# A graph attention over source nodes rewritten: keys spread by a load, scores by a broadcast weight, one-hots that carry the edge weight

## What is computed

```python
feat = jnp.concatenate([x[src], edge_weights, x[dst]], axis=1)      # 64 + 16 + 64 = 144
h = jax.nn.relu(feat @ W_att1.T + b_att1)                            # 144 wide
scores = (h @ W_att2.T + b_att2)[:, 0]
m = jax.ops.segment_max(scores, src, num_segments=num_nodes)
e = jnp.exp(scores - m[src])
denom = jax.ops.segment_sum(e, src, num_segments=num_nodes)
msg = jax.ops.segment_sum(e / denom[src] * lin_x[dst], src)          # shortened
```

## Time and profile before

| | |
|---|---|
| median of 3 runs | 28473.26 us (28471.0 to 28478.49) |
| profiled execution | 28469.76 us, span of its trace 28468.0 us |
| loop of the third layer | first gather at 16447.7 us, last at 23092.7 us |
| granted PE clock, all of the program | 0.526 of full speed |

### The profile page before, as it was taken

The page is one execution under the profiler, slowest core; times in us unless marked ns, Lnnn a source line. Parts: engine busy times, 40 slices in busy tenths (PEclk is TensorE's granted clock), DMA queues, the critical chain, the costliest instruction groups (busy, mean ns, idle before and its releaser), DMA issues. The chain is left out here.

```text
span 28468.0 us, 536803 instructions
## 1 busy us (share of the span) xinstructions
PE 20925.5 (74%) x110220; PEld 13694.9 (48%) x110221; DVE 18578.8 (65%) x61786; ACT 7653.1 (27%) x22583; POOL 16681.5 (59%) x18097
## 2 busy tenths in 40 slices
PE   0007888888888769999999789999999983333333
PEld 0004444444444445555556466666666643333332
DVE  7997888888888754544445577777777763333333
ACT  0003333333333312222222134444444421111111
POOL 0005777777777647777776345555555526777772
PEclk9655555555555555555555555555555555555555
DMA  6002222222222523333333532233322332222234
GB/s 268 0 1 42 44 44 44 44 44 44 44 44 44 43 48 76 75 76 76 76 76 69 46 80 79 78 78 79 78 79 79 78 40 60 60 60 60 60 58 22
DMA packets 2623392, 1771.81 MB, mean 62 GB/s; under 512 B 1867500, under 2 KB 2227922, under 8 KB 2616226
## 3 DMA queue, kind: packets, MB, share of 16 engines
q0 software_dynamic: 606880, 853.20, 16.4%
q1 hardware_dynamic: 2016466, 918.12, 13.6%
HBM read 1456.85 MB, written 341.56 MB: 63 GB/s over the span
## 5 line engine op out<-in xcount | busy, mean ns | idle before, releaser
L718 POOL DMA_INDIRECT H<-tab,idx x3520 | 3361.0, 955 | 3267.5 <-DMA ea<-eap 2195.6
L718 POOL DMA_INDIRECT H<-tab,rs x3520 | 3357.7, 954 | 3064.0 <-DVE V L828 2185.9
L1151 POOL DMA_INDIRECT H<-tab,m_idx x3520 | 3350.9, 952 | 1654.0 <-issue 1030.5
L1323 POOL DMA_INDIRECT g_G<-tab,g_rs x3520 | 3325.1, 945 | 1631.0 <-issue 1093.4
L1385 PE MATMUL g_ps_a<-g_zr,g_oh 128*128 128x64 f32 x7040 | 1712.3, 425 | 2865.7 <-issue 2037.1
L1075 POOL DMA_INDIRECT rec<-PT,posi x3125 | 3058.9, 979 | 1276.3 <-issue 1007.0
L935 PEld LDWEIGHTS ps_a<-V,H 128*128 128x128 f32 x14080 | 2991.6, 314 | 1232.6 <-issue 1232.6
L796 DVE CUSTOM_DVE_ANT_0 junk<-ps_lb,pen 128x512 bf16<-128x512 f32 x4400 | 2900.7, 689 | 853.4 <-PE ps_lb L903 742.6
L935 PE MATMUL ps_a<-V,H 128*128 128x68 f32 (+1 forms) x14080 | 3292.0, 411 | 82.4 <-DVE V L828 25.4
L1385 PEld LDWEIGHTS g_ps_a<-g_zr,g_oh 128*128 128x128 f32 x7040 | 1567.3, 328 | 3011.2 <-issue 2228.3
L909 PE MATMUL ps_z<-w_ea,eaT 64*128 64x288 f32 (+1 forms) x5280 | 2898.8, 681 | 5.3 <-DVE za L752 3.1
(11 more groups left out here) (253 smaller groups left out, 34862.9 us busy)
## 6 DMA issues: line engine op xcount, KB each, us to landing
rs<-rec SPq DMA_DIRECT2D x880, 164.0 KB
g_rs<-rec SPq DMA_DIRECT2D x880, 164.0 KB
rec<-H SPq DMA_DIRECT2D x46, 3116.0 KB
m_row<-key SPq DMA_DIRECT2D x880, 128.0 KB
H<-startp SPq DMA_DIRECT2D x880, 128.0 KB
PT<-in_ea SPq DMA_DIRECT2D x625, 160.0 KB
H<-tab,idx POOLq DMA_INDIRECT x3520
H<-tab,m_idx POOLq DMA_INDIRECT x3520
```

The costliest lines, as they stand in the source:

```text
L718: pool.indirect_dma_start(G[:, k, t, :], None, table, bass.IndirectOffsetOnAxis(ap=idx[:, k, t, :], axis=0)).then_inc(s_g[k], 16)
L1151: pool.indirect_dma_start(G[:, k, t, :], None, tab1, bass.IndirectOffsetOnAxis(ap=idx[:, k, t, :], axis=0)).then_inc(s_g[k], 16)
L1323: pool.indirect_dma_start(G[:, k, t, :], None, tab3, bass.IndirectOffsetOnAxis(ap=rs[:, k, t, 1:2], axis=0)).then_inc(s_g[k], 16)
```

## The change

In the third layer `attention(...)` is replaced by a new function `source_attention`. What it computes is the same, except for roundings (below). Loops are unrolled by 8 (`AHEAD`), and `rs` has 8 buffers.

- **Keys.** The sort stores each key modulo 128 in the record, so no base is subtracted (in the last layer the same subtraction becomes a copy). ACT writes the keys as float32 (`lo`) and bfloat16 (`lo16`); SP stores the 1 KB of a group to DRAM (`keyc`) and loads it again, broadcast to all partitions (`row`). DVE compares that row with the partition's number: `ohN` in one instruction. The turning of the one-hots by PE, the copy from PSUM, the float32 copy and DVE's four comparisons are gone; `pen` is computed from `ohN`.
- **Scores.** Relu, product and sum over the 144 columns are one instruction with an accumulating output per piece (L1169 of the changed kernel, 4 in a group). ACT makes a bfloat16 score `hi`, and PE spreads it with 4 products whose weights are `hi`'s column repeated 128 times and whose moving operand is the identity: no turning, no copy of turned scores, no low part.
- **Maxima.** They are kept in bfloat16, so there is one part: 4 products in place of 8.
- **Values.** `V` is gone. After the exponential DVE builds the one-hots already multiplied by the weight (L1176, 4 instructions), and `node_sums` multiplies them by the gathered rows themselves, which have a column of ones behind them.
- **Copy of the edge features.** It moves from POOL to ACT.
- **Order.** The maxima of group g now stand in the same `body` as the scores of group g.

```diff
 PAD = 2 * GE
+LOW = 2.0 ** 99
+AHEAD = 8
...
-                    do(dve.tensor_scalar(base_node[:, o, a:b], ps_g[:, nt % 2, 0:b - a], float(NB), None, ALU.min))
-                    do(dve.tensor_copy(blk[:, o, a:b], base_node[:, o, a:b]))
-                    dve.tensor_scalar(base_node[:, o, a:b], base_node[:, o, a:b], float(P), None, ALU.mult).then_inc(s_tab, 1)
+                    at_least(dve, s_tab, nt - 1)
+                    do(dve.tensor_scalar(fo[:, a:b], ps_g[:, nt % 2, 0:b - a], float(NB), None, ALU.min))
+                    if o == 0:
+                        do(dve.tensor_scalar(base_node[:, 0, a:b], fo[:, a:b], float(P), None, ALU.mult))
+                    dve.tensor_copy(blk[:, o, a:b], fo[:, a:b]).then_inc(s_tab, 1)
+            dve.wait_ge(s_tab, 2 * NSL)
...
+            do(dve.tensor_scalar(keys[1], keys[1], P - 1, None, ALU.bitwise_and))
...
+        def source_attention():
...
+                rs = sbl("rs", [P, U, T, REC], I32)
+                G, oh = in_place_of_h(ctx, ("a_G", R + 1), ("a_oh", P))
+                lo = sbl("lo", [P, U, T])
+                lo16 = sbl("lo16", [P, U, T], BF16)
+                row = sbl("row", [P, 2, GE], BF16)
+                ohN = sbl("ohN", [P, SLOTS, GE], BF16)
+                z = sbl("z", [P, T, width])
+                ss = sbl("ss", [P, T])
+                hi = sbl("hi", [P, T], BF16)
+                mn = sbl("mn", [P, 1], BF16)
...
+                def edges(g, k, r):
+                    at_least(sp, s_lo, g - U + 1)
+                    at_least(sp, s_eac, g - U + 1)
+                    settle(sp)
+                    at_least(sp, s_g[k % SLOTS], (r - 1) * (16 * T * (U // SLOTS)) + (k // SLOTS + 1) * (16 * T))
+                    settle(sp)
+                    sp.dma_start(rs[:, k], rec[bass.ds(g * GE, GE), :].rearrange("(p t) c -> p t c", p=P)).then_inc(s_ld[k], 16)
+                def keys_out(g, k, r):
+                    sp.wait_ge(s_lo, g + 1)
+                    settle(sp)
+                    sp.dma_start(keyc[bass.ds(g * GE, GE)].rearrange("(p t) -> p t", p=P), lo16[:, k]).then_inc(s_out[k], 16)
+                def keys_in(g, k, r):
+                    at_least(sp, s_ohN, g - 1)
+                    settle(sp)
+                    sp.wait_ge(s_out[k], (r + 1) * 16)
+                    settle(sp)
+                    sp.dma_start(row[:, k % 2], keyc[bass.ds(g * GE, GE)].partition_broadcast(P)).then_inc(s_row[k % 2], 16)
+                def body(*at):
+                    stage(edges, 0, NG, *at, unroll=U)
+                    stage(keys_out, 1, NG, *at, unroll=U)
+                    stage(keys_in, 2, NG, *at, unroll=U)
...
+                    pool.wait_ge(s_ld[k], (r + 1) * 16)
+                    at_least(pool, s_acc, g - SLOTS + 1)
+                    settle(pool)
+                    for t in range(T):
+                        pool.indirect_dma_start(G[:, k % SLOTS, t, 0:R], None, tab2,
+                                                bass.IndirectOffsetOnAxis(ap=rs[:, k, t, 1:2], axis=0)).then_inc(s_g[k % SLOTS], 16)
...
+                def onehots(g, k, r):
+                    dve.wait_ge(s_row[k % 2], uses(k, r, 2) * 16)
+                    at_least(dve, s_me, g - SLOTS + 1)
+                    at_least(dve, s_pen, g - SLOTS + 1)
+                    settle(dve)
+                    dve.tensor_scalar(ohN[:, k % SLOTS], row[:, k % 2], pcol[:], None, ALU.is_equal).then_inc(s_ohN, 1)
+                def scores(g, k, r):
+                    dve.wait_ge(s_z, g + 1)
+                    dve.wait_ge(s_g[k % SLOTS], uses(k, r) * (16 * T))
+                    at_least(dve, s_sum, g)
+                    settle(dve)
+                    for b in range(2):
+                        ts = slice(b * tpb, (b + 1) * tpb)
+                        ins = dve.tensor_tensor(z[:, ts, :], zv[b], G[:, k % SLOTS, ts, 0:width], ALU.add)
+                    ins.then_inc(s_act, 1)
+                    dve.wait_ge(s_act, g + 1)
+                    at_least(dve, s_lg, g)
+                    at_least(dve, s_hi, g)
+                    settle(dve)
+                    for t in range(T):
+                        ins = dve.scalar_tensor_tensor(z[:, t, :], z[:, t, :], 0.0, att, ALU.max, ALU.mult, accum_out=ss[:, t:t + 1])
+                    ins.then_inc(s_sum, 1)
+                def weighted(g, k, r):
+                    dve.wait_ge(s_p, g + 1)
+                    at_least(dve, s_acc, g - SLOTS + 1)
+                    for t in range(T):
+                        ins = dve.tensor_scalar(oh[:, k % SLOTS, t, :], iota_b[:], lo[:, k, t:t + 1], p[:, t:t + 1], ALU.is_equal, ALU.mult)
+                    ins.then_inc(s_oh, 1)
...
+                def maxima(g, k, r, b):
+                    m_old = M[:, bass.ds(b, 1)]
+                    dve.wait_ge(s_lb, g + 1)
+                    dve.wait_ge(s_pen, g + 1)
+                    at_least(dve, s_mn, g)
+                    settle(dve)
+                    dve.tensor_tensor_reduce(junk[:], ps_lb[:], pen[:, k % 2], 1.0, -LOW, ALU.add, ALU.max, gm[:]).then_inc(s_gm, 1)
+                    dve.wait_ge(s_gm, g + 1)
+                    at_least(dve, s_mb, g)
+                    at_least(dve, s_me, g)
+                    settle(dve)
+                    dve.tensor_tensor(mn[:], m_old, gm[:], ALU.max).then_inc(s_mn, 1)
+                    dve.wait_ge(s_mn, g + 1)
+                    at_least(dve, s_corr, g)
+                    dve.tensor_tensor(df[:], m_old, mn[:], ALU.subtract).then_inc(s_df, 1)
+                    dve.wait_ge(s_df, g + 1)
+                    settle(dve)
+                    dve.tensor_copy(m_old, mn[:]).then_inc(s_mb, 1)
+                def exponents(g, k, r):
+                    dve.wait_ge(s_me, g + 1)
+                    dve.wait_ge(s_lg, g + 1)
+                    at_least(dve, s_p, g)
+                    settle(dve)
+                    dve.tensor_tensor(dd[:], lg[:], ps_m[:, 0:T], ALU.subtract).then_inc(s_d0, 1)
+                    dve.wait_ge(s_d0, g + 1)
+                    dve.tensor_scalar(dd[:], dd[:], 70.0, None, ALU.min).then_inc(s_d, 1)
...
+                def body(g, k, r):
+                    at = (g, k, r)
+                    stage(scores, 0, NG, *at, unroll=U)
+                    stage(weighted, 1, NG, *at, unroll=U)
+                    stage(onehots, -2, NG, *at, unroll=U)
+                    older = None
+                    if not isinstance(g, int) or g >= 2:
+                        older = blocks[k - 2] if k >= 2 else block_of(g - 2)
+                    if not isinstance(g, int) or g < NG:
+                        blocks[k] = block_of(g)
+                        maxima(g, k, r, blocks[k])
+                    if older is not None:
+                        keep(g - 2, (k - 2) % U, r + (k - 2) // U, older)
+                    stage(exponents, 0, NG, *at, unroll=U)
...
+                def spread(g, k, r):
+                    pe.wait_ge(s_hi, g + 1)
+                    at_least(pe, s_gm, g)
+                    for t in range(T):
+                        mm = pe.matmul(lbv[:, t, :], hi[:, t:t + 1].broadcast_to([P, P]), identb[:], start=True, stop=True)
+                    mm.then_inc(s_lb, 1)
+                def edge_maxima(g, k, r):
+                    pe.wait_ge(s_mn, g + 1)
+                    at_least(pe, s_d0, g)
+                    for t in range(T):
+                        mm = pe.matmul(ps_m[:, t:t + 1], ohN[:, k % SLOTS].rearrange("n (p t) -> n t p", t=T)[:, t, :], mn[:],
+                                       start=True, stop=True)
+                    mm.then_inc(s_me, 1)
+                def node_sums(g, k, r):
+                    pe.wait_ge(s_oh, g + 1)
+                    at_least(pe, s_done, g)
+                    for t in range(T):
+                        mm = pe.matmul(ps_a[:, 0:VC], oh[:, k % SLOTS, t, :], G[:, k % SLOTS, t, v0:R + 1],
+                                       start=(t == 0), stop=(t == T - 1))
+                    mm.then_inc(s_acc, 1)
+                def body(*at):
+                    stage(feature_rows, -1, NG, *at, unroll=U)
+                    stage(turn, -2, NG, *at, unroll=U)
+                    stage(spread, 0, NG, *at, unroll=U)
+                    stage(key_rows, -1, NG, *at, unroll=U)
+                    stage(edge_maxima, 0, NG, *at, unroll=U)
+                    stage(node_sums, 1, NG, *at, unroll=U)
...
+                def local_keys(g, k, r):
+                    act.wait_ge(s_ld[k], (r + 1) * 16)
+                    at_least(act, s_oh, g - U + 1)
+                    settle(act)
+                    act.copy(lo[:, k], rs[:, k, :, 0])
+                    at_least(act, s_out[k], r * 16)
+                    settle(act)
+                    act.copy(lo16[:, k], rs[:, k, :, 0]).then_inc(s_lo, 1)
...
+                def penalty(g, k, r):
+                    act.wait_ge(s_ohN, g + 1)
+                    at_least(act, s_gm, g - 1)
```

(19 more changed lines are left out.)

132 lines of the change are left out of this document (130 added, 2 removed).

## The result

The changed kernel takes 28540 us (median of 20 runs, 28510 to 28567), the kernel before 28473 (20 runs, 28468 to 28478). The ratio is 1.0023, with a 95% interval of 1.0016 to 1.0030. I had forecast 27540, and 26950 to 27930 as the range. The kernel is 1000 us slower than forecast, and a little slower than before. In the runs e5 to e12 every kernel, that before too, took some 26% longer, so each of them is given by its ratio to the runs of before beside it and compared with its neighbours alone.

The account below looks back on a forecast made before the run. PE at 1.2 GHz was taken as the bound: 7.57 us a group falls to 6.50, saving 942 us over 880 groups, with 9 us added: 28469.76 - 942 + 9 = 27537, stated as 27540, range 26950 to 27930.

Parts of the forecast that it names:

- PE is the bound, and DVE has room: Third layer's loop: PE at 1.2 GHz sets the pace, 6.43 us of its own work a group after the change.
- DVE's sum: DVE's work in a group after the change: 5.74 us of pieces and some 0.1 for waits, about 5.85.
- PE has `node_sums` until 5.6 + 1.87 = 7.45: Round trip of one group: node_sums follows the edges' maxima at 5.6 us, so PE is last, by 0.3 us.
- I cost all of these at nothing: Changes on ACT, POOL, SP and in transfers within the loop were taken to add no time.
- "cover" of two groups: Loads of records and keys are issued two groups, about 12.5 us, ahead of need; an uncrowded load took 2.5.
- I take 0.45: PE's four spread products of 128 columns: 0.45 us a group, from L878's 0.38 to next start and 0.59 alone.
- The clock: PE's granted clock in the third loop was expected to stay at 0.50 to 0.55.
- 6.50 forecast: Time for a group of the third loop: PE's list of 6.43 us plus 0.07 for groups with missed waits.
- Dear accumulating operations: Rival: accumulators cost DVE its rate, making it the bound, 6.9 us a group, 27890 us; 0.18, including unseen waits.
- Full clock: Rival: PE gets 2.4 GHz for most of the loop, DVE's 5.85 us sets the pace, 26965 us; chance 0.11.
- Late transfers: Rival: records or keys land after their two-group lead, holding ACT, DVE and PE; up to 29700 us; chance 0.09.
- The slower side: Program time longer than before the change, beyond the 0.2% counted as no change; chance 0.07.

Follow-up runs that it names:

- e5: The changed kernel with rows of the gathered tile G padded from 836 to 896 bytes; ratio 1.0139.
- e12: The changed kernel with two buffers for node_sums, unrolled by 4 in place of 8, and bfloat16 keys made one group earlier; ratio 0.9862.
- e17: The changed kernel unrolled by 4 in place of 8, with ACT making the bfloat16 keys one group earlier; 28153 us, ratio 0.9889.
- e16: The changed kernel with two buffers in turn for the sums of node_sums; 28393 us, ratio 0.9965.
- e13: The kernel of e12 run again (changed kernel, two sum buffers, unrolled by 4, keys early); 27987 us, ratio 0.9827.
- e15: The kernel of e14 with DVE's keep put ahead of maxima; 27982 us, ratio 0.9826.
- e1: The changed kernel unrolled by 4 in place of 8, copies three groups ahead in place of five, SP loading keys before storing; 29394 us, ratio 1.0322.
- e3: The changed kernel with DVE's keep put ahead of maxima; 28337 us, ratio 0.9953.
- e14: The kernel of e13 with PE's turn moved behind spread; 27978 us, ratio 0.9826.

## Why the prediction was wrong

- **PE is the bound, and DVE has room: right for the work.** Save for the spread, PE's pieces went as listed. DVE's sum held, but partly by luck: read by starts in one group of the changed kernel (from 19000.45) 0.96 + 0.92 + 1.03 + 0.35 + 2.11 + 0.45 = 5.82 us, against 5.85. Inside it the four accumulating operations came out at 0.92, the lower bound, and not at 1.33 (below), and the additions (0.82 forecast), the weighted one-hots (0.91) and the maxima through `keep` (1.88) were each dearer by 0.12 to 0.23. And PE was no longer busy without a break: 80% of the loop where I wrote above 95%, with DVE at 67% where I wrote 88%.
- **"PE has `node_sums` until 5.6 + 1.87 = 7.45": this step failed first.** I let `node_sums` start right behind the edges' maxima. It has a second wait, `at_least(pe, s_done, g)`, on the `keep` that DVE does only after the maxima, with one buffer in PSUM. I listed everything that DVE does in that stretch and never asked which of it PE's last piece waits for. The wait is 0.82 us in every group; what it costs is 0.19.
- **The loops unrolled by 8 and "I cost all of these at nothing": the dearer omission.** Unrolling did not appear in my sum at all. It costs 0.50 us a group, and 387 or 406 us of the program's time (changed kernel to e17, e16 to e13). My range had no case for it. The "cover" of two groups that I named did hold for transfers; it says nothing of an engine that has no instructions to execute.
- **"I take 0.45" for the four products of the spread: mis-sized.** They take 0.75 at 1.2 GHz and 0.41 at 2.4 GHz (19042.02 to 19042.43 in e15). The row that I took it from, four products with four different weights of the same size at 1.2 GHz, was 0.38 before. The two differ in more than the repeated column: the spread writes float32, to every fourth place of its row in PSUM (`lbv`), and L878 writes bfloat16 side by side. Which of these doubles the time was not tested. That is 0.30 us for a group at 1.2 GHz, at most 264 us.
- **The clock gave some back.** I forecast 0.50 to 0.55 and it was 0.62. PE was busy for 6.09 us a group in place of 6.43, in spite of the dearer spread, since more groups ran at 2.4 GHz.
- **The sum by groups:** 6.50 forecast; the spread +0.30; what e13 has beyond that +0.13, unexplained; the wait for the sums +0.19; the stop +0.50. That is 7.62. It is an account at the mean clocks that these kernels had, and these moved with each edit (0.60 to 0.65).
- **The rivals.** Dear accumulating operations (0.18): wrong, they are cheap. Full clock (0.11): a small part, 0.62 and not 1. The rule of the Trainium skill that I weighed there (TensorE: Matmul & The Clock Gate, What's actually happening), that activity releases the throttled state, still has the trace against it: at 95% busy the clock was 0.55, at 80% it is 0.62. Late transfers (0.09): not in this kernel, but right next door, in e1, at 8.56 us a group. The slower side got 0.07, and it happened by a way that was on no list.

## What to carry to other kernels

Before an unrolled loop is costed, count an engine's instructions in one turn of it and look at the instruction queue of the trace: here 176 or 188 of DVE's ran without a fetch, and 342 or 366 cost 2.8 or 5.1 us at every jump back. For each piece of the engine that bounds, write down all its waits, those for a free buffer too, and find where in its neighbour's order the releasing instruction stands. And read a wait as an upper bound of what its removal brings: one of 0.82 us a group was worth 0.19, because the next wait stood right behind it, while a stop of 0.64 us a group (421.2 by 656) was worth 0.50. Where the granted clock is not at one level, look at it beside every comparison of orders: in e3, e14 and e15 the waits changed as meant, and the share of the work that ran at 2.4 GHz changed with them.
